# Adding the base and the selected rows on GpSimd and VectorE instead of TensorE

## The chip, the cores and the metric

One core of one Trainium2 chip runs the whole program. The metric is the device time of one execution in microseconds. The profile abbreviates the engines: PE is TensorE (PEld its weight loads), DVE is VectorE, ACT is ScalarE, POOL is GpSimd, SP is SyncE.

## What is computed

`x` is [32, 256, 128]: 32 blocks of 256 rows. It is normalised to `xn`, and `out = x + attention(xn) + ffn(xn)`.

```
q, k, v = heads(xn @ Wq), heads(xn @ Wk), heads(xn @ Wv)          # 16 heads of 8, within a block of 256 rows
qc, kc  = q - mean(q), k - mean(k)
scores  = qc @ kc.T / 8 + var(q)[:, None] * var(k)[None, :] / 8
attention = merge(softmax(scores) @ v) @ Wo
ffn: causal attention over the 32 sequences, residual, layer norm,
     then the top 2 of 8 experts for each token, added to the residual
```

## The kernel before

The program has three phases. In the first, 16 groups of 512 tokens go through the causal attention and the router of the feed-forward part. It writes two things to memory: `out_base`, which is x plus the residual stream, and each token's row once for each of its two experts, scattered by indirect DMAs of GpSimd. The features of attention's blocks 0 and 1 are made at its end. In the second phase the experts run over 40 blocks of 512 gathered rows and write `expert_out`. The third phase, where the change lies, is the attention over the 32 blocks of 256 rows.

The third phase is a software pipeline written out by hand. Each engine has a function `step(b, p)` (p is the parity of the block, for double buffers), and steps run from b = -1 to 32. In step b the engines work on five blocks at once: the outputs of block b-1 (`prev`), scores, exponentials and products with V of block b (`cur`), the second half of the transposed features of b+1 (`nxt`), the first half of b+2 (`prep`), and normalisation, projection and features of b+3 (`norm`). A step has 16 slots h, one for each head. The tables `PE_AT`, `DVE_AT` and `ACT_AT` say in which slot an engine does each of its side jobs. All engines run in order, so a wait holds everything behind it on that engine. The engines meet through semaphores only.

For each head PE computes scores twice: once with queries in the rows, from which DVE takes the maxima (L1249), and once transposed, from which ACT takes the exponentials (L1684). `row_pass` reuses one of three banks as soon as DVE has taken an older maximum. PE then multiplies the exponentials with V.

The features of a block are its queries and keys in 8 columns of `feat` plus a 9th with a scaled sum of squares, which makes the variance term part of the same product. They are split into a high and a low half precision part in `stack`, where each head has a row of 32 places: high, a copy, and the rest (`FEAT` is 9, `D` is 8, `parts` and `slots` are views of `stack`). ScalarE copies the projection from PSUM to `feat` (`features`, L1655), in slot 9. GpSimd then squares it and adds in a tree (`features_squares`, L507 to L515), scales into the 9th column (L519), casts all 9 columns to the high part (L522, `features_high`), and, in the next step, copies the high part twice (L527) and subtracts it (L529, `features_low`). PE's `stack_transposes` of that block wait for L529, in slot 9 of the step, and `project_qk` of block b+3 stands right behind them in PE's order. ScalarE's `features` of b+3 waits for that.

GpSimd also fetches, by four indirect DMAs a block (`gather`, L620), the two expert rows of each of a block's tokens: `gather(p, k, st)` fetches choice k of half st into `ysel[p][:, k, st]`. In the order of POOL's step b: `scale_x` (L495, L497), `add_selected` of block b-1 (L626, adds the two choices), a small instruction (L616) that follows the waits of `gather_ready`, the first gather, `features_low`, the second gather, `features_squares`, the third gather, `features_high`, the fourth gather.

The output of a block is put together in PSUM. In slot 13, `project_out` multiplies the merged attention `oT_all` with `wo` and adds `base_t` (the block's rows of `out_base`, loaded by SP) and `ysel[p][:, 0]` by products with the identity, in one accumulation. ScalarE's `take_output` copies the bank to `z_out` in slot 14 (L1668), and SP stores that.

The traces name some tiles otherwise than the code: all PSUM banks are `bank`, and `ysel` is `xg`, whose memory it uses. Matmuls that go through the helper `mm` all have line L726.

## Time and profile before

| | us |
|---|---|
| three runs | 1019.8, 1020.74, 1021.52 (median 1020.74) |
| the profiled execution | 1018.14, its span 1016.5 |
| busy in the span | PE 891.7, DVE 811.5, ACT 686.9, POOL 617.0 |
| groups of tokens | up to about 375 |
| experts | about 375 to 524 |
| attention | about 524 to 1016.5 |

Shares of busy time are averages over three phases with different limits. What a change in the third phase does is to be read from that phase. A matmul's end is modelled in these profiles, so consecutive matmuls overlap in the records, and what counts is the distance between starts. The granted clock of TensorE is 1.00 at full speed (2.4 GHz) and 0.50 at the lower level (1.2 GHz).

### The profile page before, as it was taken

What the parts mean: (1) busy time and instruction counts of PE and PEld (TensorE: products, weight loads), DVE (VectorE), ACT (ScalarE), POOL (GpSimd) and SP (SyncE); (2) the same over time, 40 slices, a digit from 0 to 9 for tenths busy, and PEclk for the clock granted to TensorE, in tenths of its full rate; (3) what the DMA queues carried; (4) which work ended last, traced back from release to release, by engine and by line L of the source; (5) the groups of instructions that cost most, each with busy time, mean ns of one, the idle gap of its engine ahead of it and who ended that gap; (6) DMA issues with size and microseconds to landing.
All of it is one profiled execution on the core that took longest, in us unless ns stands there. A gap on an engine that the chain in (4) does not pass through costs nothing.

```text
span 1016.5 us, 33829 instructions
## 1 busy us (share of the span) xinstructions
PE 891.7 (88%) x11984; PEld 558.3 (55%) x12001; DVE 811.5 (80%) x2182; ACT 686.9 (68%) x1395; POOL 617.0 (61%) x886
## 2 busy tenths in 40 slices
PE   6788877878886469999999999999999999999997
PEld 2555555545554337887864555555555555555543
DVE  7788978988887575655569889999999999999880
ACT  4687877778883224434457777787787787787775
POOL 4157656667666851222228777787787777777751
PEclk9888989999998659999999999999999999999999
DMA  5613323332311245777721111111111111111111
GB/s 150 94 41 77 88 70 82 97 78 69 80 46 31 51 143 157 221 227 224 228 86 38 47 50 40 43 50 40 42 50 40 42 50 40 45 51 38 41 48 33
DMA packets 110939, 80.56 MB, mean 79 GB/s; under 512 B 23408, under 2 KB 98032, under 8 KB 110832
## 3 DMA queue, kind: packets, MB, share of 16 engines
q1 hardware_dynamic: 99440, 51.78, 20.0%
q0 software_dynamic: 11392, 27.35, 8.6%
q8 instruction: 68, 1.11, 0.5%
q14 instruction: 39, 0.32, 0.1%
HBM read 44.83 MB, written 33.73 MB: 77 GB/s over the span
## 4 chain that ended last, share of the span: by engine, by line
PE 41%; POOL 21%; issue 14%; DVE 11%; ACT 10%; SPq 1%; DMA 1%; POOLq 0%; DVEq 0%; ACTq 0%
PE bank L726 35%; POOL xg L620 4%; POOL stack L529 3%; ACT Vexp L1728 2%; PE bank L765 2%; DVE rowmin L1249 2%; POOL stack L527 2%; POOL sq L507 2%; PE bank L1052 2%; POOL rstd L495 2%; POOL token_rows L565 1%; ACT gxb L1756 1%; POOL sq L509 1%; POOL stack L522 1%; ACT rows L1771 1%
## 5 line engine op out<-in xcount | busy, mean ns | idle before, releaser
L1249 DVE TENSOR_REDUCE rowmin<-bank 128x2 f32<-128x512 f32 x512 | 326.7, 683 | 36.0 <-PE bank L726 35.9
L1684 ACT ACTIVATE prob<-bank 128x512 f32<-128x512 f32 x512 | 290.2, 602 | 79.4 <-PE bank L726 79.2
L726 PE MATMUL bank<-QKT 32*128 32x256 f16 x2048 | 183.8, 275 | 19.6 <-DVE rowmin L1249 16.7
L565 POOL DMA_INDIRECT token_rows<-rows,spots x128 | 125.8, 983 | 40.6 <-issue 32.8
L620 POOL DMA_INDIRECT xg<-expert_out,place x128 | 128.0, 1000 | 33.0 <-POOL spare L616 9.2
L726 PEld LDWEIGHTS bank<-QKT 32*128 32x128 f16 x2048 | 66.9, 93 | 131.9 <-issue 48.8
L726 PE MATMUL bank<-prob,V 128*25 128x256 f32 x2048 | 136.4, 384 | 0.4 <-ACT prob L1684 0.4
L1843 ACT ACTIVATE hmid<-bank,wrow,up_scale 128x512 f32<-128x512 f32 x80 | 58.0, 774 | 86.2 <-PE bank L726 86.2
L640 POOL DMA_DIRECT2D expert_out<-y x40 | 30.2, 755 | 116.6 <-DVE y L1561 109.6
L726 PEld LDWEIGHTS bank<-prob,V 128*25 128x25 f32 x2048 | 50.3, 103 | 51.6 <-issue 26.2
L726 PE MATMUL bank<-wrow,hmid 128*128 128x128 f32 x640 | 77.8, 275 | 0.0
L726 PEld LDWEIGHTS bank<-wrow,hmid 128*128 128x128 f32 x640 | 74.6, 192 | 0.1
L1551 DVE CAST turned<-bank 128x512 f16<-128x512 f32 x40 | 27.7, 692 | 45.5 <-PE bank L1052 45.5
L726 PE MATMUL bank<-turned,wrow 128*128 128x512 f16 x240 | 59.6, 385 | 3.0 <-DVE turned L1553 3.0
L507 POOL TENSOR_TENSOR sq<-feat 128x512 f32<-128x512 f32 x32 | 33.3, 1041 | 47.6 <-ACT feat L1655 47.6
L1294 DVE TENSOR_REDUCE smax<-bank 128x16 f32<-128x512 f32 x64 | 43.8, 684 | 18.1 <-PE bank L726 18.1
L726 PE MATMUL bank<-hnT,in_wT 128*128 128x512 f32 x64 | 38.2, 681 | 19.0 <-ACT hnT L1699 14.5
L726 PE MATMUL bank<-Kexp,gqT 32*32 32x128 f32 x2048 | 41.2, 315 | 11.2 <-issue 11.1
L550 POOL TENSOR_TENSOR rstd<-var,minus_half 128x4 f32<-128x4 f32 x16 | 16.6, 1037 | 55.6 <-DVE minus L1341 55.6
L1305 DVE STREAM_TRANSPOSE sprobT<-prob 128x512 f32<-128x512 f32 x64 | 43.5, 697 | 8.1 <-ACT prob L1735 7.8
L726 PE MATMUL bank<-causal,onesb 128*128 128x512 bf16 x184 | 48.4, 386 | 1.1 <-issue 0.2
L1240 DVE COPY QKT<-bank 128x1024 f16<-128x1024 f16 x64 | 43.5, 680 | 5.2 <-PE bank L765 5.2
(229 smaller groups left out, 1913.9 us busy)
## 6 DMA issues: line engine op xcount, KB each, us to landing
xrow<-token_rows SPq DMA_DIRECT2D x40, 258.0 KB, 3.2
wrow<-weight_rows SPq DMA_DIRECT2D x40, 257.0 KB, 3.3
expert_out<-y POOLq DMA_DIRECT2D x40, 256.0 KB, 2.8
token_rows<-xrow SPq DMA_DIRECT2D x16, 258.0 KB, 5.8
xg<-in_L_attn_x SPq DMA_DIRECT2D x64, 64.0 KB
x_in<-in_L_attn_x SPq DMA_DIRECT2D x32, 128.0 KB
out_base<-acc SPq DMA_DIRECT2D x64, 64.0 KB
base_t<-out_base SPq DMA_DIRECT2D x32, 128.0 KB, 2.7
```

The lines of the kernel that those rows point to most:

```text
L507: pool.tensor_tensor(sq[:].rearrange(flat), eight, eight, ALU.mult).then_inc(s_pool, 1)
L529: ins = pool.tensor_tensor(slots[p][:, a, :, 2 - a, :], feat[:, a], slots[p][:, a, :, 0, :], ALU.subtract)
L565: pool.indirect_dma_start(token_rows, bass.IndirectOffsetOnAxis(spots[p][:, j:j + 1], 0), rows[p][:, k, t, :].bitcast(U32), None).then_inc ...
L620: pool.indirect_dma_start(ysel[p][:, k, st, :].bitcast(U32), None, expert_out, bass.IndirectOffsetOnAxis(place[p][:, st, k:k + 1], 0)).the ...
L640: pool.dma_start(expert_out[bass.ds(at, BLK), :].rearrange("(s p) e -> p s e", p=P), y_sb[i % YBUFS][:].bitcast(U32)).then_inc(s_yd[i % YB ...
L726: return pe.matmul(o, l, r, start=start, stop=stop, skip_group_check=True)
L1240: dve.tensor_copy(QKT[p][:, :, HALF * k:HALF * (k + 1), :], misc[0][:].bitcast(F16).rearrange("p (a g s) -> p a g s", a=2, g=HALF)).then_i ...
L1249: dve.tensor_reduce(rowmin[h // 8][:, :, h % TILE_ROWS, h // TILE_ROWS % HALF], row_scores[i % 3][:].rearrange("p (s t) -> p s t", s=ST), ...
L1294: dve.tensor_reduce(smax[:, r, :], ps, AX.X, ALU.max).then_inc(s_dve, 1)
L1305: dve.transpose(sprobT[:, r].rearrange("p h s -> p (h s)"), sprob[:, r].rearrange("p h s -> p (h s)")).then_inc(s_spT[r], 1)
L1684: act.activation(prob[:, h % 8].rearrange("p t s -> p (t s)"), col_scores[h % 2][:], ACT.Exp, scale=exp_register).then_inc(s_exp, 1)
L1843: act.activation(hmid[i % 2][c][:], up_bank[c][:], ACT.Gelu, bias=w[:, c:c + 1], scale=up_scale[:, 0:1]).then_inc(s_mid, 1)
```

## The change

- `project_out` multiplies with `wo` only; the four products with the identity go, and with them PE's waits for `s_ysum` and `s_based`.
- GpSimd gets `add_base`, which adds `base_t` to choice 0 of the expert rows once the first two gathers have landed. It stands between `features_squares` and the third gather. `add_selected` adds choice 1 as before, in the next step.
- `take_output` moves from ScalarE to VectorE (slot 14) and adds `ysel[p][:, 0]` to the bank while it copies.
- ScalarE's `features` copies the projection a second time, cast, straight into the first 8 columns of the high part. The first copy now signals `s_full`, the second `s_feat`. In GpSimd's `features_high` only the 9th column is cast.
- `features_low` makes its two copies of the high part in one instruction.
- `gather_ready` waits for `s_z` instead of `s_pr_ps`, and SP's `load_base` for `s_ysum`.

```diff
-DVE_AT = dict(half1=1, out=5, half0=10, statistics=0, shift1=12, shift0=3)
+DVE_AT = dict(half1=1, out=5, half0=10, statistics=0, shift1=12, shift0=3, output=14)
...
             def features_squares(n):
 
-                pool.wait_ge(s_feat, n + 1)
-                if positive(n - 1):
-                    pool.wait_ge(s_half_ps[1], n - 1)
-                if isinstance(n, int) and n == 0:
-                    pool.wait_ge(s_zeroed, 1)
+                pool.wait_ge(s_full, n + 1)
...
                 pool.wait_ge(s_pool, own.next())
+                pool.wait_ge(s_feat, n + 1)
                 pool.tensor_tensor(sq[:, :, :, 0], sq[:, :, :, 0], sq[:, :, :, 1], ALU.add).then_inc(s_pool, 1)
...
-                pool.tensor_copy(parts[p][:, :, 0:FEAT], feat[:].rearrange(flat)).then_inc(s_pool, 1)
+                pool.tensor_copy(parts[p][:, :, D:FEAT], feat[:].rearrange(flat)[:, :, D:FEAT]).then_inc(s_pool, 1)
...
             def features_low(p):
-                for a in range(2):
-                    pool.tensor_copy(slots[p][:, a, :, 1 + a, :], slots[p][:, a, :, 0, :])
+                size = ST * H * ROWS
+                twice = bass.AP(stack[p][:].tensor, stack[p][:].offset + FEAT,
+                                [list(stack[p][:].ap[0]), [size + FEAT, 2], [ROWS, ST * H], [1, FEAT]])
+                pool.tensor_copy(twice, slots[p][:, :, :, 0, :])
...
                 pool.wait_ge(s_placein[p], n * 16 + (32 - 16 * p))
                 if positive(n - 1):
-                    pool.wait_ge(s_pr_ps, n - 1)
+                    pool.wait_ge(s_z, n - 1)
...
+            def add_base(n, p):
+                pool.wait_ge(s_based[p], n * 8 + (16 - 8 * p))
+                pool.wait_ge(s_sel[p], n * 32 + (32 - 32 * p))
+                pool.tensor_tensor(ysel[p][:, 0], ysel[p][:, 0], base_t[p][:], ALU.add).then_inc(s_pool, 1)
+                pool.wait_ge(s_pool, own.next())
...
                 if second:
+                    add_base(b - 1, 1 - p)
                     gather(1 - p, 1, 0)
                     gather(1 - p, 1, 1)
...
                 if norm:
                     features_squares(b + 3)
                 if cur and not early:
+                    add_base(b, p)
                     gather(p, 1, 0)
...
                 pe.wait_ge(s_oa, b + 1)
-                pe.wait_ge(s_ysum, b + 1)
-                pe.wait_ge(s_based[p], b * 8 + (16 - 8 * p))
                 for st in range(ST):
                     to = misc[0][:, st * P:(st + 1) * P]
-                    mm(to, oT_all[:, st * P:(st + 1) * P], wo[:], stop=False)
-                    mm(to, ident[:], base_t[p][:, st], start=False, stop=False)
-                    ins = mm(to, ident[:], ysel[p][:, 0, st], start=False)
+                    ins = mm(to, oT_all[:, st * P:(st + 1) * P], wo[:])
...
+            def take_output(b, p):
+                dve.wait_ge(s_pr_ps, b + 1)
+                dve.wait_ge(s_ysum, b + 1)
+                if positive(b * 8 - 8 * p):
+                    dve.wait_ge(s_out[p], b * 8 - 8 * p)
+                dve.tensor_tensor(z_out[p][:], misc[0][:, 0:NS].rearrange("p (s e) -> p s e", s=ST), ysel[p][:, 0],
+                                  ALU.add).then_inc(s_z, 1)
...
-            def features(n):
+            def features(n, p):
                 act.wait_ge(s_qk_ps, n + 1)
                 if positive(n):
                     act.wait_ge(s_stack, n)
                 act.copy(feat[:].rearrange(flat)[:, :, 0:D],
+                         x_bank(n)[:].rearrange("p (g d) -> p g d", d=D)).then_inc(s_full, 1)
+                if positive(n - 1):
+                    act.wait_ge(s_half_ps[1], n - 1)
+                if isinstance(n, int) and n == 0:
+                    act.wait_ge(s_zeroed, 1)
+                act.copy(parts[p][:, :, 0:D],
                          x_bank(n)[:].rearrange("p (g d) -> p g d", d=D)).then_inc(s_feat, 1)
...
-            def take_output(b, p):
-                act.wait_ge(s_pr_ps, b + 1)
-                if positive(b * 8 - 8 * p):
-                    act.wait_ge(s_out[p], b * 8 - 8 * p)
-                act.copy(z_out[p][:].rearrange("p s e -> p (s e)"), misc[0][:, 0:NS]).then_inc(s_z, 1)
...
             def load_base(b, p):
                 if positive(b - 1):
-                    sp.wait_ge(s_pr_ps, b - 1)
+                    sp.wait_ge(s_ysum, b - 1)
```

## Rows read from the trace of the kernel before

**Rows 1.** Busy time by stretch: stretch, its length, each engine's, clock, DMA.
```profile
core 0: us, PE busy (x) PEld busy (x) DVE busy (x) ACT busy (x) POOL busy (x), PEclk, DMA share, GB/s
562.00:977.00 415.00, 402.82 (x4792) 222.37 (x4793) 376.38 (x810) 320.39 (x702) 321.98 (x487) 1.00 0.16 44
```
**Rows 2.** Waits from 600 to 900 us, for POOL and for PE.
```profile
engine line waited for: us in total, times, longest us
POOL sq L507 <- ACT feat L1655: 24.6, 20, 1.3
POOL xg L626 <- DMA xg<-expert_out,place: 11.8, 20, 0.7
...
PE bank L765 <- POOL stack L529: 2.5, 10, 0.3
```
**Rows 3.** POOL in order of time: start, duration, instruction, idle time before.
```profile
549.13 1.04 POOL L507 TENSOR_TENSOR sq<-feat 128x512 f32<-128x512 f32 x1
...
960.72 1.04 POOL L507 TENSOR_TENSOR sq<-feat 128x512 f32<-128x512 f32 x1 [1.22 <-ACT feat L1655]
```
**Rows 4.** All engines in order of time, the step that ends at 594.
```profile
588.99 0.73 POOL L626 TENSOR_TENSOR xg<-xg 128x256 f32<-128x256 f32 x1 [1.81 <-DMA xg<-expert_out,place]
...
593.55 1.01 PE L765 MATMUL bank<-identh,stack 128*128 128x128 f16 x8 [1.45 <-POOL stack L529]
```
**Rows 5.** Groups of instructions by shape, 620 to 920 us: busy, mean; idle before.
```profile
L527 POOL COPY stack<-stack 128x288 f16<-128x288 f16 x40 | 17.3, 480 | 0.3
...
L626 POOL TENSOR_TENSOR xg<-xg 128x256 f32<-128x256 f32 x20 | 14.5, 725 | 11.9 <-DMA xg<-expert_out,place 11.9
L522 POOL CAST stack<-feat 128x576 f16<-128x576 f32 x20 | 14.5, 723 | 1.4
...
L519 POOL TENSOR_SCALAR feat<-sq,var_scale 128x64 f32<-128x64 f32 x20 | 11.8, 591 | 0.9
...
L1272 DVE TENSOR_TENSOR o_nat<-bank,rsum 128x256 f32<-128x256 f32 x20 | 8.5, 424 | 0.7
```
**Rows 6.** The chain of waits, between L507 and L509.
```profile
704.13 0.07 issue
```
**Rows 7.** Groups of instructions by shape on POOL, whole span.
```profile
L481 POOL CAST identh<-ident 128x128 f16<-128x128 f32 x1 | 0.3, 290 | 0.1
```
**Rows 8.** All engines in order of time, 702 to 707 us.
```profile
702.33 0.59 ACT L1655 COPY feat<-bank 128x512 f32<-128x512 f32 x1 [0.54 <-PE bank L726]
...
704.03 0.33 PEld L726 LDWEIGHTS bank<-QKT 32*128 32x128 f16 x8 [0.69 <-DVE rowmin L1249]
...
704.20 0.73 POOL L509 TENSOR_TENSOR sq<-sq 128x256 f32<-128x256 f32 x1
704.22 0.73 DVE L1259 SCALAR_TENSOR_TENSOR shift<-rowmin,shift 128x16 f16<-128x16 f32 x1
...
704.90 0.39 PE L726 MATMUL bank<-base_t,ident 128*128 128x128 f32 x2
...
705.12 0.39 PE L726 MATMUL bank<-xg,ident 128*128 128x128 f32 x2
...
706.06 0.98 POOL L620 DMA_INDIRECT xg<-expert_out,place  x1 [0.27 <-POOL sq L515]
...
706.78 1.29 DVE L1249 TENSOR_REDUCE rowmin<-bank 128x2 f32<-128x512 f32 x2 [0.62 <-PE bank L726]
```
**Rows 9.** POOL in order of time, step 1.
```profile
540.75 0.95 POOL L620 DMA_INDIRECT xg<-expert_out,place  x1 [0.30 <-issue]
...
542.91 1.02 POOL L620 DMA_INDIRECT xg<-expert_out,place  x1 [0.16 <-issue]
```
**Rows 10.** The chain of waits, last group before the experts.
```profile
350.43 0.73 POOL stack L522
```
**Rows 11.** All engines in order of time, steps 29 to 31.
```profile
978.96 1.29 DVE L1249 TENSOR_REDUCE rowmin<-bank 128x2 f32<-128x512 f32 x2 [1.01 <-PE bank L726]
...
992.28 0.60 ACT L1684 ACTIVATE prob<-bank 128x512 f32<-128x512 f32 x1 [0.98 <-PE bank L726]
...
1006.46 0.60 ACT L1684 ACTIVATE prob<-bank 128x512 f32<-128x512 f32 x1 [2.24 <-PE bank L726]
```
**Rows 12.** Busy time by stretch, around the disturbed step; columns as in rows 1.
```profile
593.00:597.00 4.00, 3.44 (x20) 2.39 (x20) 0.93 (x3) 0.70 (x3) 1.40 (x2) 0.57 0.13 33
```

More of the change, by code:

```diff
@@ L372, in attention_and_experts_kernel @@
         s_feat = sem("s_feat")
+        s_full = sem("s_full")
         s_v_ps = sem("s_v_ps")
@@ L1583, in step @@
                         normalise_out(b - 1)
+                    if h == DVE_AT["output"] and prev:
+                        take_output(b - 1, 1 - p)
                     if h == DVE_AT["half0"] and prep:
@@ L1819, in group_step @@
                 if isinstance(g, int) and g == GROUPS - 1:
-                    features(1)
+                    features(1, 1)
                 if norm:
@@ L1829, in group_step @@
                 if isinstance(g, int) and g == GROUPS - 2:
-                    features(0)
+                    features(0, 0)
                 if norm:
@@ L1859, in step @@
                     if h == ACT_AT["features"] and norm:
-                        features(b + 3)
+                        features(b + 3, 1 - p)
                     if h == ACT_AT["shift1"] and cur and not (isinstance(b, int) and b == 0):
@@ L1866, in step @@
                         merged_out(b - 1)
-                    if h == ACT_AT["output"] and prev:
-                        take_output(b - 1, 1 - p)
                     if h == ACT_AT["shift0"] and nxt:
```

## The prediction

> **What bounds the kernel now.** I read four views in this order. The busy time by stretch comes first: between 562 and 977 us, where 27 of the 32 blocks of attention pass, PE is busy for 403 of 415 us, DVE for 376, ACT for 320 and POOL for 322 [rows 1]. Read alone, it says that PE is the bound and that taking matmuls off it pays. It can't say so: the modelled end of a matmul overlaps the start of the next, and a wait can hide in between.
>
> So second, the waits by engine over 300 us, about 20 steps [rows 2]. POOL waited for ScalarE's copy of the features 20 times, 24.6 us in all: 1.23 us once in each step. PE waited in ten of them for L529, POOL's last instruction on the stack, 0.25 us each (stack_transposes waits there for oT_all too, and its weight loads carry the other ten). POOL also waits 0.59 us a step for the landing of its last gather.
>
> Third, GpSimd's instructions in order of time [rows 3]. L507, the squares of the features, starts at 549.13 and, 27 steps later, at 960.72: 15.24 us a step, some 15.15 without the 2.5 us that one disturbed step lost. The idle time ahead of L507 is 1.23 us on the average of 20 steps and 1.3 at most [rows 2]. That it never varies is the finding. From the end of L529 the way goes to PE (stack_transposes, project_qk), to ACT (features) and back to POOL (L507). In that time POOL does one gather, 1 us, and then waits its 1.23: some 2.4 us with the gaps. From L507 to L529 it runs its own program, the other 12.7 us. The two make a closed ring. If another engine set the step, the 1.23 would vary.
>
> Fourth, the one disturbed step shows how tight the ring is [rows 4]: a gather landed late, L626 waited 1.81 instead of 0.59 us, and PE waited 1.45 us for L529. Of the extra 1.22 us on POOL, 1.20 reached PE. So PE, DVE and ACT are about 0.25 us ahead of POOL at that point: GpSimd bounds, with little behind it.
>
> **The change, part by part.** What counts in a step is POOL's program from L507 on.
>
> 1. *add_base, new on POOL*, after the squares and before gather(p, 1, 0), so inside the ring. It has the shape and a tile of add_selected: L626, 725 ns [rows 5]. The handshake with its own semaphore behind it costs 0.07 us [rows 6]. Its two other waits (s_based, s_sel) and the new one on s_feat stand behind such handshakes, where nothing hides them; a wait that is already met must be cheaper than the whole handshake, so between 0 and 0.07 each. I take 0.03, 0.10 in all. What they wait for is there: SP asks for base_t early in the step, and gather(p, 0, 1) starts ahead of L507, 5 us before add_base. Together **+0.90 us**, from +0.80 to +1.0.
>
> 2. *features_high*: L522 casts 576 elements in 723 ns; 64 are left, one in each row of 32. The nearest rows are L522 and the cast of 128 elements, L481, 0.290 us [rows 5, 7]: 0.97 ns an element between them, so 0.23 us at 64. Below, half of L481 is 0.15; above, L519 takes 591 ns for 64 strided elements with a scalar from a tile. I take 0.23, since a plain copy is nearest to the casts. **-0.50 us**, from -0.13 to -0.57.
>
> 3. *features_low*: two copies of 288 elements at 480 ns, which overlap by about 0.1 us, become one of 576. That should cost what L522 does, 0.72. **-0.15 us**, from 0 to -0.25.
>
> The ring grows by 0.90 - 0.50 - 0.15 = **+0.25 us a step** (from nothing to +0.87 with all bounds at one end). From L507 of step 1 to L529 of step 29 it is passed 28 times: +7.0 us.
>
> 4. *features on ScalarE*: the copy to feat, on which POOL starts, comes as before. The second one, 0.59 us like the first at 702.33 [rows 8], delays two exponentials by 0.5 us. PE needs the first of them for head 12, by about 704.0, and was held by DVE until 704.03; head 13 comes 0.2 us later. PE gets 0.88 us back a moment after that, so nothing remains. s_feat then fires 2 us before POOL asks for it. The z_out copy leaves ACT.
>
> 5. *project_out*: 4 of 6 matmuls go, which are 8 of 12 records, since a float32 matmul runs as two. A pair starts 0.22 us after the one before [rows 8]: **0.88 us** of PE a step. Inside the ring this is worth nothing: it lies between project_qk and the next L529, for which PE has to wait anyway. It pays where the ring is open (part 6).
>
> *take_output* on DVE reads PSUM and one tile in SBUF, as L1272 does in 424 ns [rows 5]. It stands ahead of the maximum of slot 14, where DVE waits 0.62 us for PE, from 706.16 to 706.78 [rows 8]. With project_out shorter, DVE does it there and goes on at 706.6. The price is hidden; without that cover it is 0.42 us of DVE.
>
> DVE can be held by GpSimd, too: at 704.22 L1259, with two inputs in SBUF, took 0.73 us and ended with POOL's L509, which had started at 704.20 [rows 8]. The new add_base starts at about 705.9, 0.15 ahead of where the third gather starts now, and is still running when DVE comes to take_output. If that holds DVE as L1259 was held, it is 0.5 us late. DVE is idle 1.4 us a step [rows 1], so the ring hides even this.
>
> The Trainium skill (SBUF — State Buffer, Who interferes with whom) says that a VectorE instruction with two inputs in SBUF contends with a GpSimd one that reads SBUF, and that one with a single such input doesn't. By it take_output, with its other input in PSUM, keeps its 0.42 us, and DVE is 0.2 us ahead of where it is now. The trace agrees for L1259 and shows no case like take_output beside an add on POOL.
>
> *Queues*: SP's load_base waits for an earlier event than before, and gather_ready for an s_z that fired half a step before. Nothing new queues behind either.
>
> 6. *Outside the ring.* **Ramp:** in step 1 add_base(0) must await the landing of the gather started at 540.75 [rows 9]. With the 0.65 saved on POOL in step 0 that one is usable at 542.8 (gathers here take about 2.65 us from start to use), the add and its handshakes take 1.0, and the next gather starts at 543.8 instead of 542.91: +0.9 us. **Before the experts:** features_high of block 1 is on the chain that leads on to the scatters and the experts' blocks [rows 10]: -0.65 us. **Tail** (steps 29 to 32, without features, PE leading) [rows 11]: at 978.96 DVE waits 1.01 us behind project_out, of which take_output uses 0.42: -0.5. At 992.28 ACT waits 0.98: -0.88. At 1006.46 ACT waits 2.24, project_out having run at half the clock: twice 0.88, so -1.7. The last project_out is on the path to the end: -0.88, less 0.05 for DVE's 0.42 in place of ACT's 0.37: -0.8. Together -3.9 us.
>
> **Sum:** 7.0 + 0.9 - 0.65 - 3.9 = +3.35 us on the profiled execution's own 1018.14 us (span 1016.5): 1021.5. The median of the runs shown, 1020.74, is 2.6 higher: 1024.1, say 1024.0.
>
> **The rivals.**
> - *POOL saves as much as it adds.* With the column copy at 0.15, the merged copy at 0.60 and the waits at nothing, the step grows by 0.80 - 0.57 - 0.25, which is nothing, and only -3.65 us remain outside the ring: 1017.1. It is a faster kernel from a growth below 0.06 us a step and no change between 0.06 and 0.20. For it: both copies are extrapolated. Against: the new add alone is measured, and 0.15 would be a copy without any fixed cost. Chance of faster this way 0.09.
> - *PE is the real bound.* Then its 0.88 us would show, at most by the 0.25 us that separate it from POOL: 27 x 0.25 + 3.9 = 10.7 us less, 1010. Against it stands the constant 1.23. Chance 0.04.
> - *DVE becomes the bound.* It works 13.7 of 15.15 us and gets 0.42 more. If add_base holds take_output (0.5) and the splits of shift0, now closer behind L626, are held by another 0.35, DVE is 1 us worse with the 0.42 counted, and PE comes later to the transposes than POOL. Ring plus 0.3: 28 x 0.55 + 0.9 - 0.65 - 3.9 = +11.7 us, 1032.4. It decides from about 0.7 us of new hold: 0.25 that PE waits now, 0.25 of longer ring, 0.2 gained at 706.6. Chance 0.08.
> - *The clock.* Between 593 and 597 the granted clock is 0.57, right after PE's wait of 1.45 us [rows 4, 12]; 4 us at 0.57 lose 1.7. In the new kernel PE waits longer for POOL in every step: 0.25 now, 0.25 more from the ring, and up to 0.88 from its lighter work. If four more steps fall to 1.2 GHz: +6.8 us, 1030.8. Against: it fell once in 27 steps, behind the longest wait of all. Chance 0.09.
>
> **How the numbers follow.** 0.2% of this kernel is 2.0 us, about what a measurement can tell from no change. My case (growth of 0.12 to 0.45 us a step, so -0.3 to +9 us) has 0.70, of which 0.18 lies below +2.0. Faster: 0.09 + 0.04 = 0.13. Same: 0.18, and 0.02 of the first rival's edge: 0.20. Slower: 0.52 + 0.08 + 0.07 of the clock: 0.67. The likeliest case's own range is 1020.5 to 1029.5. For 8 in 10 the range goes down to 1018.8, where the first rival begins, and up to 1031.5, between the clock's case and DVE's.
>
> **What would show it.** From L507 to L507 15.4 us instead of 15.15, with 1.2 us idle ahead of it still; the copy of 64 elements at 0.23 us and the merged one at 0.72; a new POOL add of 0.725 ahead of the third gather; PE's wait for L529 up from 0.25 to 0.5 us or more; take_output at 0.42 us on DVE; from the last L507 to the end 3.9 us less. I am wrong if the idle time ahead of L507 varies (then another engine sets the step), if the column copy costs what L519 does, or if the clock falls inside the ring.

## The result, and the profile after

| | us |
|---|---|
| kernel before, four runs beside it | 1019.8 to 1024.55, median 1021.13 |
| changed kernel, four runs | 1034.21 to 1039.78, median 1037.76 |
| ratio | 1.017, interval 1.0134 to 1.0205 |
| profiled execution of the changed kernel | 1038.53, its span 1036.9 |

The change makes the kernel 1.7% slower, about 16.6 us. The prediction had the sign, but 3.35 of the 16.6 us, and a range that ended at 1031.5. Every comparison below is a ratio to runs of the kernel before on the same chip, whose medians there lie between 1015.1 and 1021.1. One profiled execution, of the version with both adds behind the second gather, was a disturbed one (1027.58 us; three of that version's ten runs were, and its ratio leaves them out), but its clock falls only behind 944 us, and all that is read from it lies ahead of that.

The lines have new numbers: the squares are L504 (were L507), the cast of features_high L520 (L522), features_low L527 and L529 as before, add_base L627, add_selected L632, stack_transposes L773 (L765), the split of the row minima L1261 and L1263 on DVE (L1257 and L1259), take_output L1273.

The squares of steps 1 and 28, POOL in order of time, answer to [rows 3]:

```profile
553.40 1.03 POOL L504 TENSOR_TENSOR sq<-feat 128x512 f32<-128x512 f32 x1
...
982.01 1.04 POOL L504 TENSOR_TENSOR sq<-feat 128x512 f32<-128x512 f32 x1 [1.22 <-ACT feat L1669]
```

Between them lie 27 periods. They took 411.6 us before, 15.24 each, and take 428.6 now, 15.87 each: +17.0 us. The first of them starts 4.3 us later than before, and the end follows the last after 54.9 instead of 55.8 us. So +4.3, +17.0 and -0.9 make the 20.4 us between the two spans, and the attention's inner steps are the place to look.

The waits from 600 to 900 us, which answer to [rows 2]:

```profile
POOL sq L504 <- ACT feat L1669: 23.4, 19, 2.0
PE bank L773 <- POOL stack L529: 19.1, 19, 1.4
...
POOL xg L632 <- DMA xg<-expert_out,place: 11.2, 19, 0.7
...
POOL xg L627 <- POOL sq L513: 4.8, 19, 0.3
```

PE now waits in every step for POOL's L529, 1.0 us where the record had 0.25 in every second one. POOL's own waits are what they were, 1.2 us for the features and 0.59 for the landing. That is the picture of the closed ring, with POOL later and PE waiting for it.

One step of POOL and of DVE beside it, in order of time (start, duration, instruction, idle time before):

```profile
712.31 1.04 POOL L504 TENSOR_TENSOR sq<-feat 128x512 f32<-128x512 f32 x1 [1.15 <-ACT feat L1669]
713.43 0.72 POOL L506 TENSOR_TENSOR sq<-sq 128x256 f32<-128x256 f32 x1
...
715.27 0.73 POOL L627 TENSOR_TENSOR xg<-xg,base_t 128x256 f32<-128x256 f32 x1 [0.25 <-POOL sq L513]
715.31 0.41 DVE L1273 TENSOR_TENSOR z_out<-bank,xg 128x256 f32<-128x256 f32 x1
```

and the groups of POOL instructions by shape, 620 to 920 us, which answer to [rows 5]:

```profile
L527 POOL COPY stack<-stack 128x576 f16<-128x576 f16 x19 | 14.7, 774 | 0.3
...
L627 POOL TENSOR_TENSOR xg<-xg,base_t 128x256 f32<-128x256 f32 x19 | 13.9, 730 | 4.8 <-POOL sq L513 4.8
...
L520 POOL CAST stack<-feat 128x64 f16<-128x64 f32 x19 | 9.0, 471 | 1.3
```

The add costs 0.73 and the gap ahead of it 0.25, together +0.98 us. The cast of 64 elements takes 0.47, which is 0.25 less than the cast of 576 and not 0.50 less. The merged copy takes 0.77; from its start to that of L529 it is 0.74 us where it was 0.83, so -0.09. These three make +0.64 us a step. Measured over the 23 periods without a stretch of lowered clock it is 15.70 against 15.15, +0.55: the idle time ahead of the squares is alternately 1.15 and 1.22 instead of 1.22 and 1.23, which gives back 0.04, and 0.05 us is not attributed.

28 passes of 0.55 are 15.4 us, most of the loss. The rest of the 17.0 between the squares is in four periods of 16.5 to 17.4 us, against one such before. In each of them the granted clock falls. Busy time by stretch, in two of the four places (columns as in rows 1), and PE's wait just ahead of each:

```profile
631.40:634.80 3.40, 3.40 (x21) 1.65 (x24) 1.74 (x3) 1.62 (x4) 1.38 (x2) 0.50 0.08 19
914.70:918.10 3.40, 3.40 (x24) 1.80 (x24) 1.46 (x3) 1.34 (x3) 1.25 (x2) 0.50 0.07 19
```
```profile
630.82 0.61 PE L773 MATMUL bank<-identh,stack 128*128 128x128 f16 x8 [1.36 <-POOL stack L529]
...
914.27 0.65 PE L773 MATMUL bank<-identh,stack 128*128 128x128 f16 x8 [1.39 <-POOL stack L529]
```

0.50 is 1.2 GHz. PE's waits for L529 in the changed kernel alternate between steps of 0.4 to 1.0 us and steps of 1.3 to 1.6. The four drops follow waits of 1.36, 1.39, 1.60 and 2.36 us; nine other waits from 1.28 to 1.57 us were followed by none. So in this trace the clock fell behind waits of this size, but not behind each of them. Ahead of the fall in [rows 12], too, PE had waited 1.45 us [rows 4].

### The profile page after: what moved, and what is told of

Read it like the earlier page. It is cut to its first block, busy times and chain, and to the rows that moved or that the text cites. A ratio compares the mean times of both kernels' runs of the same rounds, so it can differ in the third digit from the quotient of the medians.

```text
span 1036.9 us, 33400 instructions
## 1 busy us (share of the span) xinstructions
PE 880.6 (85%) x11728; PEld 532.8 (51%) x11745; DVE 821.0 (79%) x2214; ACT 694.1 (67%) x1395; POOL 628.8 (61%) x886
## 4 chain that ended last, share of the span: by engine, by line
POOL 32%; PE 31%; issue 15%; ACT 11%; DVE 8%; SPq 1%; POOLq 1%; DMA 1%; ACTq 0%; DVEq 0%
PE bank L734 27%; POOL xg L620 8%; POOL stack L529 4%; POOL sq L504 3%; ACT Vexp L1742 3%; POOL stack L527 2%; POOL sq L506 2%; POOL rstd L496 2%; POOL xg L627 2%; PE bank L773 2%; PE bank L1056 2%; POOL feat L517 2%; ACT feat L1669 2%; ACT gxb L1770 2%; POOL token_rows L565 1%
## 5 line engine op out<-in xcount | busy, mean ns | idle before, releaser
L1698 ACT ACTIVATE prob<-bank 128x512 f32<-128x512 f32 x512 | 287.5, 605 | 58.8 <-PE bank L734 54.9
L734 PE MATMUL bank<-QKT 32*128 32x256 f16 x2048 | 190.9, 278 | 28.0 <-DVE rowmin L1253 22.7
L734 PE MATMUL bank<-prob,V 128*25 128x256 f32 x2048 | 139.8, 392 | 0.0
L773 PE MATMUL bank<-identh,stack 128*128 128x128 f16 x512 | 41.6, 227 | 30.9 <-POOL stack L529 30.6
L504 POOL TENSOR_TENSOR sq<-feat 128x512 f32<-128x512 f32 x32 | 33.2, 1039 | 52.3 <-ACT feat L1669 52.3
L734 PE MATMUL bank<-hnT,in_wT 128*128 128x512 f32 x64 | 40.7, 720 | 19.9 <-ACT hnT L1713 15.0
L1669 ACT COPY feat<-bank 128x512 f32<-128x512 f32 x32 | 18.7, 585 | 54.3 <-PE bank L734 54.3
L773 PEld LDWEIGHTS bank<-identh,stack 128*128 128x128 f16 x512 | 30.5, 100 | 46.5 <-issue 34.2
L550 POOL TENSOR_TENSOR rstd<-var,minus_half 128x4 f32<-128x4 f32 x16 | 16.6, 1037 | 55.8 <-DVE minus L1353 55.8
```

The costliest lines, as they stand in the source:

```text
L504: pool.tensor_tensor(sq[:].rearrange(flat), eight, eight, ALU.mult).then_inc(s_pool, 1)
L734: return pe.matmul(o, l, r, start=start, stop=stop, skip_group_check=True)
L773: ins = pe.transpose(m[:, a, g, st], stack[p][:, a, st, h:h + TILE_ROWS, :].rearrange("p h k -> p (h k)"), identh[:])
L1669: act.copy(feat[:].rearrange(flat)[:, :, 0:D], x_bank(n)[:].rearrange("p (g d) -> p g d", d=D)).then_inc(s_full, 1)
L1698: act.activation(prob[:, h % 8].rearrange("p t s -> p (t s)"), col_scores[h % 2][:], ACT.Exp, scale=exp_register).then_inc(s_exp, 1)
```

## The experiments

**The two halves of the change, each alone.** The output part (adds only) is the kernel before with add_base, take_output on DVE and project_out without the identity products; the features part is the changed kernel without these.

```diff
 # adds only: the kernel before, and
+                    add_base(b, p)                      # ahead of gather(p, 1, 0), L527 twice and L522 whole as before
-                    mm(to, ident[:], base_t[p][:, st], start=False, stop=False)
-                    ins = mm(to, ident[:], ysel[p][:, 0, st], start=False)
```

> The kernel before with only the output part of the change: add_base on GpSimd, project_out with wo alone, take_output on VectorE; the features are made as before. Ring theory (GpSimd's program from the squares to the rest of the stack sets the step): the changed kernel's trace prices the add at 0.73 us and the gap ahead of it at 0.25, so the step grows from 15.15 to about 16.1 us; with 28 passes and about 3 us less in the tail the time is some 25 us above before, ratio 1.02 to 1.03, and more than the full change costs. Clock theory (the loss comes from TensorE falling to 1.2 GHz because it has less to do): the same work has gone from TensorE as in the full change, so the same loss, ratio 1.010 to 1.018.

> The kernel before with only the features part: ScalarE casts 8 columns into the stack, GpSimd casts the 9th and makes one doubling copy; no add_base, the identity products stay. Ring theory: 0.25 + 0.09 us less on GpSimd a step, of which the other engines let through about 0.25 (their lead in the kernel before): 27 x 0.25 is 7 us less, ratio 0.992 to 0.996. Clock theory: no change of TensorE's work, so ratio 1.00, or a little less than that. If ScalarE's second copy of 0.59 us were the cost: ratio above 1.00.

The adds alone: 1060.17 us, ratio 1.043 (1.0357 to 1.0504). Its undisturbed periods are 16.03 us, where the ring asks for 15.15 + 0.98 = 16.13. The mean is 16.6, because the granted clock falls in 12 places of the ring, 48 us in all at 0.50. The mean granted clock from 562 to 977 us is the last figure but two:

```profile
562.00:977.00 415.00, 370.97 (x4184) 188.73 (x4182) 357.43 (x770) 291.52 (x622) 313.13 (x475) 0.94 0.15 41
```

Its PE waits 1.4 us for L529 in 16 steps. So the adds cost more than the whole change, and about 0.6 us a step of that is the clock. Neither theory had the time (1.02 to 1.03, and 1.010 to 1.018): the undisturbed step is the ring's, the rest is the clock's.

The features alone: 1022.55 us, ratio 1.0069 (1.0036 to 1.0102), with no fall of the clock in the ring. GpSimd's program is 0.34 us shorter in it, yet the periods are 15.1 or 15.6 us, 15.39 on the average, and the idle time ahead of the squares varies from 1.3 to 2.2 us. POOL no longer sets the step, and the 0.992 to 0.996 that was expected did not come. What sets it is to be seen in VectorE's split of slot 3. In 15 of the 27 periods it takes 0.76 to 0.84 us, PE waits for it, and the period is 15.59 to 15.68; in the other 12 it takes 0.17 to 0.25, and the period is 15.26 at most. One step of each kind, all engines in order of time:

```profile
634.37 1.03 POOL L620 DMA_INDIRECT xg<-expert_out,place  x1 [0.28 <-POOL spare L616]
634.72 0.78 DVE L1259 SCALAR_TENSOR_TENSOR shift<-rowmin,shift 128x16 f16<-128x16 f32 x1
635.42 0.77 POOL L527 COPY stack<-stack 128x576 f16<-128x576 f16 x1
635.65 0.27 PE L848 MATMUL bank<-identh,shift 128*16 128x128 f16 x2 [0.43 <-DVE shift L1259]
...
712.95 0.17 DVE L1259 SCALAR_TENSOR_TENSOR shift<-rowmin,shift 128x16 f16<-128x16 f32 x1
713.76 0.78 POOL L527 COPY stack<-stack 128x576 f16<-128x576 f16 x1
```

The split is long where it meets POOL's gather, and ends just behind the start of the merged copy. The experiments below take this hold up. In the steps without it the others need 15.12 us, level with POOL before; whether ScalarE's second copy has a part in that, no run isolates.

**Refilling TensorE.** In the changed kernel the products with wo are made three times; the first two results are overwritten by the last. PE gets its 0.88 us back and the ring stays.

```diff
-                    ins = mm(to, oT_all[:, st * P:(st + 1) * P], wo[:])
+                    for _ in range(3):
+                        ins = mm(to, oT_all[:, st * P:(st + 1) * P], wo[:])
```

> The changed kernel with each product with wo in project_out done three times over into the same place, so that TensorE has as many records a step as before (the result is that of the last). Ring theory: inside the ring nothing changes, the step stays at 15.7 us; the tail gives back its 3 us; ratio to before 1.015 to 1.02. Clock theory: with TensorE as busy as before the clock stays up and most of the loss goes: ratio 1.00 to 1.008.

1031.89 us, ratio 1.0187 (1.0141 to 1.0233), undisturbed periods 15.68. TensorE's relief buys nothing in the ring. The changed and the refilled kernel were later run side by side:

> The changed kernel itself, beside the next one on the same chip. Theory of the ring: a ratio near 1.017, undisturbed steps of 15.70 us as before, so 15.4 us over 28 steps. Theory of the clock: some of the remainder comes from stretches of the granted clock at half speed (four in the ring in the profile after), so it is slower than the kernel with refilled products by 0.3 to 0.7%.

> The changed kernel with the products with wo made three times, as once before, now beside the changed kernel on one chip. If TensorE's lighter work had no part in the loss: undisturbed steps 15.70, and a total 3 us longer, for the tail then has no relief. If it costs the clock: fewer stretches at half speed (0 or 1 in the ring against 3 or more), and a total 2 to 6 us shorter.

The changed kernel: 1041.29 us, ratio 1.0193 (1.0151 to 1.0235), 15.71 us undisturbed. Refilled: 1036.95, ratio 1.0158 (1.0117 to 1.0199), 15.73 undisturbed. The medians differ by 4.3 us in the direction of the clock's theory, but the intervals overlap. The profiles are clearer. In the changed kernel PE waits for L529 up to 1.7 us once the second step is over; in the refilled one it waits 0.31 and 0.22 in turn. A step of the changed kernel in order of time, and then the refilled one's waits from 600 to 900 us:

```profile
758.07 0.93 PE L773 MATMUL bank<-identh,stack 128*128 128x128 f16 x8 [1.40 <-POOL stack L529]
```
```profile
PE bank L773 <- POOL stack L529: 5.1, 19, 0.3
```

The clock falls in five places of the ring, each behind a wait of 1.27 us or more, and in one, behind the only long wait that the refilled kernel has (2.43 us, in the second step). The 27 periods take 3.5 us less refilled, the tail 54.6 instead of 59.0 us. So a lighter TensorE gains nothing here, and by these two profiles it loses some of the clock; the times alone don't separate the two kernels.

**The same adds where GpSimd waits anyway.** POOL idles 1.2 us for the features behind its second gather. If the ring is all, an add of 0.73 us moved there leaves it.

```diff
 # before, window: in POOL's step
-                if prev and not second:
-                    add_selected(b - 1, 1 - p)          # was ahead of the first gather
...
                     gather(p, 0, 1)
-                if second:
+                if prev:
                     add_selected(b - 1, 1 - p)
                 if norm:
                     features_squares(b + 3)
```

> The kernel before with add_selected of block b-1 moved in GpSimd's order: from the start of step b (where it waits 0.59 us for a gather to land and takes 0.73) to behind the second gather, where GpSimd is idle for 1.23 us anyway. Nothing else. Ring theory: the ring loses 1.3 us and another engine sets the step after the first 0.25 us or so; 7 us less, ratio 0.990 to 0.995, and GpSimd's idle time ahead of the squares is now long and varies. If TensorE set the step already: ratio 1.00. If the others were further ahead than the 0.25 us that I read: down to 0.975.

1079.9 us, ratio 1.0642 (1.0602 to 1.0682): slower where all three readings had it the same or faster. All engines in order of time, where the first gather starts:

```profile
747.21 1.03 POOL L620 DMA_INDIRECT xg<-expert_out,place  x1 [0.49 <-POOL spare L616]
747.85 0.58 DVE L1255 TENSOR_SCALAR shift<-rowmin 128x16 f16<-128x16 f32 x1
748.25 0.89 POOL L527 COPY stack<-stack 128x288 f16<-128x288 f16 x2
748.46 0.70 DVE L1257 SCALAR_TENSOR_TENSOR shift<-rowmin,shift 128x16 f16<-128x16 f32 x1
...
749.32 0.27 PE L846 MATMUL bank<-identh,shift 128*16 128x128 f16 x2 [0.75 <-DVE shift L1257]
```

With add_selected gone from their front, the first gather and features_low come earlier against DVE, just onto the two small splits of the row minima. Each takes 0.17 us when nothing on POOL meets it (175 ns on the average in the protected version below); here the one ends 0.2 us behind the gather that began before it, the other with the copies, and PE waits for them (21.0 us in 17 steps from 600 to 900). Undisturbed periods are 15.98 us, and 11 falls of the clock, 65 us, bring the mean to 17.14.

The Trainium skill (SBUF — State Buffer, Who interferes with whom) says that VectorE and GpSimd contend for a shared pair of ports when a tensor_scalar enters a two-port mode, or when an instruction of VectorE has two inputs in SBUF and the one of GpSimd reads SBUF. The second split, which has two such inputs, agrees with it: 0.70 us against 0.17. Whether the first, a tensor_scalar that took 0.58, enters such a mode, no run here shows.

To test that hold, POOL waits for the split (s_shift[0]) ahead of the small instruction in front of the first gather, so that they cannot meet:

```diff
+                if split:
+                    pool.wait_ge(s_shift[0], n + 2)
                 pool.tensor_tensor(spare[:], epsilon[0:1, 0:1], epsilon[0:1, 0:1], ALU.add).then_inc(s_pool, 1)
```

> The kernel before with add_selected in GpSimd's idle time, which alone cost 6.4 per cent, and GpSimd's wait for the split. Hold theory: that loss came from VectorE's splits, held for 0.58 to 1.37 us by gathers and copies of GpSimd, TensorE waiting for them and falling to 1.2 GHz; with the wait both go, and the step is at or a little below 15.1 us: ratio 0.985 to 1.002. If something else cost the 6.4 per cent (the late sum for project_out, say): still 1.04 or more.

1039.53 us, ratio 1.0172 (1.014 to 1.0205), no fall of the clock in the ring, a period of 15.74. That lies between what the two theories expected. 4.7 of the 6.4% are gone, though POOL waits 34.8 us in 19 steps for the split, and PE again waits for L529, 0.95 and 0.55 us in turn. The hold is shown as the cause of most of the loss; the second split of a step (slot 12, 0.65 us) is not protected and stays slow.

**The changed kernel with both adds behind the second gather**, without and with that wait:

```diff
-                    add_base(b, p)                      # was behind the squares
...
+                    add_base(b - 1, 1 - p)              # behind the second gather
                     add_selected(b - 1, 1 - p)
```

> The changed kernel with both adds of block b-1 (base, then choice 1) behind the second gather of step b, in GpSimd's idle time ahead of the squares. Ring theory: 0.98 and 0.72 + 0.59 us leave the ring, and the two adds overfill the idle time of 1.2 us by about 0.5: GpSimd needs some 14.0 us a step and VectorE, with 14.2 us of work, or TensorE sets it at 14.6 to 14.9; 8 to 14 us below before, ratio 0.985 to 0.993. Clock theory: TensorE still has less to do, so the loss stays: ratio above 1.00.

> The changed kernel with both adds in GpSimd's idle time, and GpSimd waits, ahead of the small instruction in front of the first gather, until VectorE has split the shifts of slot 3. Without the wait the step was 15.36 us, GpSimd's instructions ran while VectorE did its two small splits, and those took 0.65 and 0.69 us instead of 0.17 each; TensorE waited 1.06 us for them. Hold theory (a GpSimd instruction keeps VectorE's waiting): the splits go back to 0.17 us, the wait costs GpSimd about 0.9 us of which its idle 1.34 us takes most, and the step falls to 14.4 to 14.8 us; ratio 0.97 to 0.985. Ring theory alone (VectorE's or TensorE's work sets 15.36): the step stays, ratio 1.00. If GpSimd's added wait binds: longer than 15.4 us.

Without the wait: 1018.91 us (the median of all ten runs), ratio 0.9982 (0.9939 to 1.0025). Its first two periods are 13.88 and 14.01 us, and then it falls into a rhythm of 15.36, not the 14.6 to 14.9 that was expected, in which both splits are held (all engines in order of time):

```profile
711.22 1.03 POOL L620 DMA_INDIRECT xg<-expert_out,place  x1 [0.51 <-POOL spare L616]
711.71 0.65 DVE L1258 TENSOR_SCALAR shift<-rowmin 128x16 f16<-128x16 f32 x1
712.26 0.77 POOL L527 COPY stack<-stack 128x576 f16<-128x576 f16 x1
712.39 0.69 DVE L1260 SCALAR_TENSOR_TENSOR shift<-rowmin,shift 128x16 f16<-128x16 f32 x1
...
713.22 0.27 PE L849 MATMUL bank<-identh,shift 128*16 128x128 f16 x2 [1.06 <-DVE shift L1260]
```

With the wait: 1008.3 us, ratio 0.9872 (0.9822 to 0.9923), a period of 15.00 and no fall of the clock in the ring. The split L1262 is 0.175 us on the average of 39, L1260 0.286. The gain of 0.36 us a step is less than the hold theory's (14.4 to 14.8): the wait takes 22.3 us in 20 steps, POOL has no idle time left ahead of the squares, and PE waits for L529 again, 0.99 and 0.50 us in turn, so POOL sets the step. The adds of this change are affordable, then; their place in POOL's order made them cost.

**Half of the adds.** PE keeps wo and the base rows, DVE adds the selected rows while it copies, and GpSimd has the program of before. First in place, then with add_selected behind the second gather, then with the wait as well, then with the merged copy instead of the wait.

```diff
-                pe.wait_ge(s_ysum, b + 1)
...
-                    mm(to, ident[:], base_t[p][:, st], start=False, stop=False)
-                    ins = mm(to, ident[:], ysel[p][:, 0, st], start=False)
+                    ins = mm(to, ident[:], base_t[p][:, st], start=False)
```

> The kernel before with take_output on VectorE adding the selected rows and TensorE keeping wo and the base; add_selected stays where it was. GpSimd's program is that of before. Ring theory: GpSimd's ring sets 15.15 us whatever TensorE and VectorE save: ratio 0.997 to 1.003, the gain of the tail only. If TensorE set the step, 0.44 us less on it gives 14.7 to 14.9 us: ratio 0.985 to 0.99. If the clock falls because TensorE has less to do: above 1.005.

> The kernel before with add_selected in GpSimd's idle time, take_output on VectorE adding the selected rows, and TensorE keeping wo and the base (half of the identity products). Features as before. Ring theory: GpSimd needs 13.9 us a step; TensorE loses 0.44 us, VectorE gets 0.42; the step is 14.6 to 14.9 us: ratio 0.985 to 0.993, like the full change with both adds moved. If VectorE's 0.42 us is what binds then: no better than add_selected moved alone.

> The 14.6 us kernel (add_selected in GpSimd's idle time, half of the identity products, take_output on VectorE) with the same wait of GpSimd for the split. There the second split was held by 0.25 to 0.5 us. Hold theory: it takes 0.17 us, and the step shortens by at most those 0.3 us if GpSimd, idle for 1.07 us, can take the wait: 14.3 to 14.6 us, ratio 0.975 to 0.985. Otherwise the same or a little longer than without the wait.

> The version in which TensorE keeps the base rows, VectorE adds the selected rows and add_selected stands behind the second gather (14.62 us a step), and now with the two copies of features_low in one. Theory of the ring: GpSimd still sets the step there, its idle time ahead of the squares being constant; from the start of the copy to the subtraction 0.74 us instead of 0.83, so 14.53 us a step and 2.5 us less in all, near 0.983 of the kernel before. Rival, that DVE or PE set the step there: no change of the step, 14.6.

| | median us | ratio | period us |
|---|---|---|---|
| add_selected in its place | 1018.12 | 0.9959 (0.9929 to 0.999) | 15.18 |
| behind the second gather | 1001.7 | 0.9854 (0.9773 to 0.9936) | 14.62 |
| the same, and the wait | 1022.52 | 1.0019 (0.9998 to 1.004) | 15.32 |
| the same, and the merged copy | 1009.32 | 0.9897 (0.9859 to 0.9935) | 15.01 |

The first row confirms the ring, though its ratio lies just under the 0.997 to 1.003 that was expected: with fewer products on TensorE, the period is that of before, the idle time ahead of the squares 1.22 and 1.23, and PE's wait for L529 has grown to 0.35 us a step. The second beats the kernel before and the changed one. What sets 14.62 there isn't isolated; VectorE is busy for 377 of the 388 us from 562 to 950 and is the nearest candidate. The third contradicts the hold theory's 14.3 to 14.6: the wait costs POOL 1.4 us a step, more than the hold of 0.25 us that it removes at the one split. The fourth contradicts its expectation: GpSimd's program is shorter, and the step 0.34 us longer undisturbed (14.96). The splits by shape, first of the version without the merged copy, then with it, and PE's wait in the latter:

```profile
L1255 DVE SCALAR_TENSOR_TENSOR shift<-rowmin,shift 128x16 f16<-128x16 f32 x41 | 22.8, 556 | 1.4
```
```profile
L1257 DVE SCALAR_TENSOR_TENSOR shift<-rowmin,shift 128x16 f16<-128x16 f32 x40 | 28.6, 716 | 1.4
```
```profile
PE bank L846 <- DVE shift L1257: 8.7, 21, 0.4
```

With the merged copy the split of slot 3 is longer (0.73 us at 704.24, against 0.43 in the version without, both 0.40 us behind the start of the gather), and PE waits 0.4 us a step for it, which accounts for the 0.34. As in the features alone it ends just behind the start of the merged copy (704.97 against 704.88); why the copy lengthens a hold that begins ahead of it, no run shows. In neither of the two does PE ever wait for L529, so the ring through L529 did not set the step there, although the idle time ahead of the squares is as constant (1.03 and 1.11, or 1.41 and 1.50) as in the kernel before.

**The price of the column cast.** Seven casts were added at the end of POOL's program of the kernel before, three times over; they write to tiles that are no longer used. The kernel ran once (1035.21 us); only the durations of the casts are read.

```diff
+                for dst, src in ((dense16, thin), (dense16, wide[:, :, D]), (rows16[:, :, D], thin),
+                                 (rows16[:, :, D], wide[:, :, D]), (rows16[:, :, 0:4], wide[:, :, 0:4]),
+                                 (rows16[:, :, 0:FEAT], wide), (rows16[:, 0:32, 0:FEAT], wide[:, 0:32])):
+                    pool.tensor_copy(dst, src).then_inc(s_pool, 1)
```

> The kernel before with seven casts appended to GpSimd's program at the very end, three times over, each behind a wait for the one ahead: 64 elements dense to dense, from a stride of 9, into a stride of 32, both; 64 rows of 4; 64 rows of 9; 32 rows of 9. They measure what the copy of one column costs and why it took 0.47 us and not 0.23. If the stride of 32 half precision numbers in the destination is the cost: dense about 0.23, into the stride 0.45. If the source's stride: the second one 0.45. If the number of rows is the cost, whatever they hold: 64 rows of 1, 4 and 9 near 0.47, 0.6, 0.72, and 32 rows of 9 near 0.45. The span grows by about 9 us, which says nothing.

Groups by shape; identh is a dense destination, sq a dense source, feat one with a step of 9 elements, stack one with rows of 32:

```profile
L729 POOL CAST stack<-feat 128x576 f16<-128x576 f32 x3 | 2.2, 722 | 0.2
L729 POOL CAST stack<-feat 128x64 f16<-128x64 f32 x3 | 1.4, 462 | 0.2
L729 POOL CAST stack<-sq 128x64 f16<-128x64 f32 x3 | 1.4, 460 | 0.2
L729 POOL CAST stack<-feat 128x288 f16<-128x288 f32 x3 | 1.4, 452 | 0.2
L729 POOL CAST stack<-feat 128x256 f16<-128x256 f32 x3 | 1.3, 427 | 0.2
L729 POOL CAST identh<-feat 128x64 f16<-128x64 f32 x3 | 0.9, 291 | 0.2
L729 POOL CAST identh<-sq 128x64 f16<-128x64 f32 x3 | 0.7, 236 | 18.6 <-ACT z_out L1679 18.5
```

Dense to dense, 64 elements cost 0.236 us, which is what the prediction took. The strided source adds 0.055, the destination in 64 rows 0.224. And 256 elements in four columns of those rows cost 0.427, no more than one column; from four columns to nine it is 0.295 us more for 320 elements, 0.92 ns each. So a row costs as much with one element as with four, and above that the elements count. "The number of rows, whatever they hold" is refuted by 0.427 and 0.722 in the same 64 rows.

## Why the prediction was right or wrong

- **What bounds the kernel: right, its proof too simple.** PE's wait for L529 grew as the ring demands, the adds alone gave 16.03 against 16.13, and a lighter TensorE alone changed nothing (15.18). But "if another engine set the step, the 1.23 would vary" is false. In three versions here the idle time is constant and PE never waits for L529 (but once, ahead of the rhythm, with both adds moved); these three are locked into a rhythm with constant waits all the same. The others were also not 0.25 us ahead of POOL: in the features alone, which include ScalarE's second copy and make POOL 0.34 us shorter, steps without a held split took 15.12. What proves the ring is that both waits stand in it, POOL's for the features and PE's for L529 [rows 2], and the disturbed step [rows 4].
- **add_base, +0.90: measured +0.98.** The instruction is 0.73, the waits in a row ahead of it 0.25 instead of the 0.17 that 0.07 and 0.10 made. Within the bounds given.
- **features_high, -0.50: measured -0.25.** This is the step that failed: 0.25 of the ring's error of 0.30, while the other terms and the idle time nearly cancel. The prediction scaled by elements between a cast of 64 rows of 9 (L522) and a dense one (L481) and took 0.23; the column lies in 64 rows and costs what four columns do (0.46 and 0.427). L519, its own upper bound at 0.59 and named there as a sign of being wrong, was nearer. But the trace before also has 64 elements with a step of 8 in both inputs and the output, in float32, at 0.31:

```profile
705.48 0.31 POOL L515 TENSOR_TENSOR sq<-sq 128x64 f32<-128x64 f32 x1
```

- **features_low, -0.15: measured -0.09.** The merged copy takes 0.77, not 0.72, and L529 followed the start of the two old ones after 0.83, not 0.87.
- So the ring grew by **0.55 and not 0.25**: 28 x 0.30 = 8.4 us of the miss of 13.8.
- **ScalarE's second copy, at nothing:** in the changed kernel nothing shows of it. The features alone were 0.7% slower where POOL's saving should have gained, but the long periods there are those with a held split, so that is not its price; a run with this copy alone is missing, and up to 0.2 us of the undisturbed step (15.12 where 14.9 was expected) could be its part.
- **take_output, hidden, and perhaps held by add_base: hidden, and not held.** It took 0.41 us while L627 ran beside it (715.31 against 715.27). By the rule of the Trainium skill that the prediction quoted (SBUF — State Buffer, Who interferes with whom) it should not be held, and the trace agrees. DVE as the bound did not come about: the split L1263 has a mean of 399 ns where L1259 had 434.
- **The clock, a rival at 0.09: it came, beside the main case.** It was priced at four more falls, 6.8 us; three more than before came within the ring, at about 0.7 us each, and others in the tail. I had treated it as an alternative, though its condition, PE waiting longer, follows from the forecast itself. With PE refilled the falls go, but for one. A slip of the chances goes with it: of the clock's 0.09 only 0.07 stands under slower, and the 0.02 under same are put down to the first rival.
- **Outside the ring.** Ramp: +0.63 (17.39 against 16.76 from the squares of step 0 to those of step 1) for +0.9. Before the experts: their first stores begin at 389.42 instead of 388.43, +1.0 for -0.65. That can't be read from two profiles: in the eight profiles with the features of before this store begins between 388.43 and 397.07, and in the seven with those of the change between 386.64 and 393.01. Another 2.6 us are lost by the squares of step 0, with the clock at half speed for 6.8 us from 529. It doesn't come from the change: the same stretch and the same delay stand in 4 of 16 profiles, one of them with the features of before (half of the adds, moved, with the wait), and not in the second profile of the changed kernel. Tail: -0.9 for -3.9; the granted clock of the last 54 us is 0.88, where it was 0.97, which is some 5 us by an estimate (54 x 0.09). Busy time by stretch, the whole tail and the longest fall in it:

```profile
983.00:1037.00 54.00, 44.75 (x478) 20.79 (x478) 28.91 (x58) 33.70 (x68) 24.38 (x34) 0.88 0.15 39
1023.90:1030.70 6.80, 6.27 (x52) 2.55 (x44) 0.42 (x1) 2.64 (x5) 0.72 (x1) 0.50 0.07 19
```

The ring's growth alone, priced right, would have given 1024.0 + 8.4 = 1032.4, already above the range. The other 5.4 us of the miss are 8.7 between the two profiled executions: 2.1 in the ring, 3.0 in the tail and 2.6 ahead of step 0, all three beside a lowered clock and the last not of the change, and 1.65 before the experts, within what profiles differ by there; the ramp and the passage of the ring that lies outside the 27 periods take some 0.6 off. The range ended too low because its upper end took one rival at a time on top of an unchanged ring.

## What to carry to other kernels

When a side engine closes the ring, as GpSimd does here, work moved onto it costs its full duration plus the waits ahead of it, and the engine it was taken from gives nothing back; put the work where the side engine waits anyway (here 0.9872 instead of 1.017 with all adds and the added wait, 0.9854 with half of them). But each move on GpSimd shifts which of VectorE's instructions it meets, so look in the new trace for small ones that have grown, here from 0.17 to 0.65 us, before trusting a sum. Measure a strided copy instead of scaling by elements: here one column cost what four did. And read a constant wait as a locked rhythm only; that a pair of waits stands around the ring says more of who sets it.

## What the runs showed of the hardware

- A cast of 64 elements on GpSimd: 0.236 us dense, 0.291 with a strided source, 0.462 into 64 rows, 0.427 for four columns and 0.722 for nine columns of the same rows.
- VectorE's splits of 128x16 elements take 0.17 us alone, and 0.43 to 0.84 us in the steps read here where they meet GpSimd's indirect gather, copies or adds of the squares. In the features alone the same program had periods of 15.12 with a split of 0.17 and of 15.6 with one of 0.8.
- The granted clock fell to 0.50 in the ring 4 and 5 times in the two profiles of the changed kernel, where PE waited 1.27 us or more at one point of 13 steps; 12 times with the adds alone, where it waits 1.4 us in nearly every step; 11 times with add_selected moved, where it waits 1.2 us a step for VectorE's split and never for L529. It did not fall ahead of 944 us where PE waits 1.06 us in every step (both adds moved), nor in the ring with waits of 0.95 to 1.1 us (the three versions with the added wait), and once or never in the kernels where the waits of nearly every step are 0.5 us or less.
